# A graph transformer kernel: a longer ring of gathered rows, a step moved from GpSimd to VectorE, and TensorE's first products of the last stage issued earlier

## The reference

```python
for l in range(L):                      # L = 2
    q, k, v = (x @ W[l] + b[l] for each of q, k, v)      # (N, H, D)
    a = (q[dst] * k[src]).sum(-1) * scale
    e = exp(a - segment_max(a, dst)[dst])
    alpha = e / (segment_sum(e, dst)[dst] + 1e-16)
    agg = segment_sum(alpha * v[src], dst)
    x = agg + (x @ Ws[l] + bs[l]) + enc                  # enc: the input x
x = layer_norm(x, ln_g, ln_b)
x = relu(x @ W1 + b1) @ W2 + b2 + x
x = layer_norm(x, ln_g, ln_b)
return _layernorm(x_in + (x + enc))
```

## Time and profile before

| | |
|---|---|
| median of three executions | 2162.43 us |
| the profiled execution | 2160.31 us |
| its span (first to last instruction) | 2158.5 us |
| TensorE, matmuls | 1834.3 us busy, 85% |
| VectorE | 1824.4 us busy, 85% |
| GpSimd | 1446.1 us, 67% |
| ScalarE | 877.4 us, 41% |
| granted TensorE clock, mean | 0.937 of full |
| device memory | 242 GB/s over the span |

### The profile page before, as it was taken

One profiled execution on the slowest core, in us unless ns is written; L12 is line 12 of the kernel. 1 busy time (PEld: TensorE's weight loads), 2 busy tenths in 40 slices (PEclk: granted clock), 3 DMA queues, 4 the chain that ended last, 5 costly groups with the idle time before them and its releaser, 6 DMA issues. The chain is left out here.

```text
span 2158.5 us, 33515 instructions
## 1 busy us (share of the span) xinstructions
PE 1834.3 (85%) x7437; PEld 1392.7 (65%) x7438; DVE 1824.4 (85%) x2304; ACT 877.4 (41%) x2257; POOL 1446.1 (67%) x1417
## 2 busy tenths in 40 slices
PE   6778999998489999997889999957787878888987
PEld 5656666666267787875666666636566666676776
DVE  7659999999899998984999999998898999835554
ACT  3223333333365555552333333334666656532221
POOL 3067777777677777774777777776577777566553
PEclk9989999999699999998999999977999999998998
DMA  7588888888778888886888888886688888763321
GB/s 287 185 270 294 276 287 290 275 284 279 223 225 264 267 265 267 262 265 232 256 285 283 289 279 287 282 264 191 206 281 261 263 263 274 240 190 98 98 69 47
DMA packets 225518, 523.60 MB, mean 243 GB/s; under 512 B 39707, under 2 KB 81563, under 8 KB 225446
## 3 DMA queue, kind: packets, MB, share of 16 engines
q0 software_dynamic: 106624, 349.00, 51.7%
q1 hardware_dynamic: 115942, 168.54, 22.8%
q10 hardware_dynamic: 2880, 5.24, 0.7%
HBM read 446.94 MB, written 75.39 MB: 242 GB/s over the span
## 5 line engine op out<-in xcount | busy, mean ns | idle before, releaser
L850 POOL DMA_INDIRECT all_work<-k_rows,all_work x664 | 632.0, 952 | 217.6 <-issue 188.6
L850 POOL DMA_INDIRECT v_ring<-v_rows,coll_index x624 | 607.6, 974 | 224.5 <-issue 178.2
L1928 PE MATMUL coll_banks<-coll_ev,coll_hot 128*128 128x260 f32 x2656 | 651.3, 393 | 100.4 <-DVE all_work L2049 40.7
L1928 PEld LDWEIGHTS coll_banks<-coll_ev,coll_hot 128*128 128x128 f32 x2656 | 497.1, 193 | 228.6 <-issue 106.1
L1059 PE MATMUL score_q_ps<-score_q,score_hot 128*128 x1328 | 392.6, 420 | 89.2 <-DVE score_q L1099 56.1
L1087 DVE TENSOR_TENSOR all_work<-score_q_ps,all_work 128x1024 f32<-128x1024 f32 x332 | 404.6, 1220 | 38.7 <-PE score_q_ps L1059 20.1
L2035 DVE TENSOR_TENSOR coll_ev<-v_ring,coll_banks 128x1024 f32<-128x1024 f32 x328 | 397.9, 1214 | 11.3 <-DMA v_ring<-v_rows,coll_index 5.1
L1092 DVE TENSOR_REDUCE graph_edge<-all_work 128x1024 f32 (+1 forms) x332 | 397.8, 1209 | 0.0
L1059 PEld LDWEIGHTS score_q_ps<-score_q,score_hot 128*128 128x128 f32 x1328 | 255.6, 199 | 183.4 <-issue 132.7
L1166 ACT ACTIVATE score_hot<-score_local,all_iota_col 128x512 fp32r<-128x512 uint8 x166 | 120.0, 723 | 584.1 <-DVE all_work L1087 548.5
L2049 DVE TENSOR_TENSOR all_work<-all_work,coll_banks 128x520 f32 x354 | 244.5, 691 | 57.6 <-PE coll_banks L1928 46.5
(11 more groups left out here) (323 smaller groups left out, 2340.0 us busy)
## 6 DMA issues: line engine op xcount, KB each, us to landing
score_xt<-x_turned SPq DMA_DIRECT2D x42, 512.0 KB, 6.4
x_turned<-coll_xt SPq DMA_DIRECT2D x40, 512.0 KB, 4.4
all_work<-k_rows,all_work POOLq DMA_INDIRECT x664, 4.9
score_local<-local_dst SPq DMA_DIRECT2D x166, 64.0 KB, 6.5
x_turned<-keys_xt SPq DMA_DIRECT2D x20, 512.0 KB, 4.3
score_skip<-in_x SPq DMA_DIRECT2D x40, 256.0 KB, 4.9
v_rows<-score_v_out SPq DMA_DIRECT2D x40, 256.0 KB, 5.7
skip_rows<-score_skip SPq DMA_DIRECT2D x40, 256.0 KB, 3.8
```

Of the source, the lines that this page charges most:

```text
L850: nc.gpsimd.indirect_dma_start(rows(HALF * turn + s, first)[:, t, :], None, table, at).then_inc(arrived(HALF * turn + s, first), 16)
L1928: last = nc.tensor.matmul(sums[sum_slots[u]][:, part, :], m, ev[:, s % EVS, t, part * AGG // 2:(part + 1) * AGG // 2], start=s == 0 or t = ...
```

## The change

1. The ring of the second layer keeps 16 slots up to step 68 (SWITCH) and has 8 from there on. Which slot and which use a step has is now worked out for each step up to body 5 (STEADY), so VectorE's and ScalarE's bodies 2 to 4 are written out too, and three rounds of four halves on GpSimd. The first layer's ring and order are as they were.
2. W1 is loaded whole at the start of the stage and split in body 4 in place of body 1: ScalarE at steps 7, 9, 11 and 13, VectorE at steps 8, 10, 12 and 14. W2's load moves on SyncE's queue to behind the loop over halves 4 to 15.
3. The order in which the last stage takes the blocks is worked out between bodies 0 and 1, not ahead of body 0.
4. In each half ScalarE has gain and shift at step 5 and the high part at 6, behind the root; VectorE has the low part at 7, behind the inverse root.
5. TensorE goes on to piece 0 of h without a turning ahead of it; blocks 18 and 19 are turned ahead of pieces 1 and 2. ScalarE's first half of W2's high part moves to behind piece 1, the second to behind piece 2, and the gain and shift of block 18 to behind piece 0.
6. Twice x plus shift is one operation of VectorE (scalar_tensor_tensor over 128x2048) ahead of the second pass over a group's first pair, in place of two of GpSimd.

```diff
@@ twice x plus shift
-        def twice_enc(g):
-            pool.wait_ge(enc_in, 16 * GB * (g + 1))
-            nc.gpsimd.tensor_tensor(enc, enc, enc, ALU.add).then_inc(enc_ready, 1)
-            pool.wait_ge(enc_ready, 2 * g + 1)
-            nc.gpsimd.tensor_tensor(enc, enc, across(shift), ALU.add).then_inc(enc_ready, 1)
-            twice_enc(g)
+        def twice_enc(g):
+            dve.wait_ge(enc_in, 16 * GB * (g + 1))
+            v.scalar_tensor_tensor(enc, enc, 2.0, shift.unsqueeze(1).to_broadcast([P, GB, C]), ALU.mult, ALU.add).then_inc(enc_ready, 1)
@@ last_norms
-            dve.wait_ge(enc_ready, 2 * (g + 1))
+            if pair[0] % GB == 0:
+                twice_enc(g)
+            dve.wait_ge(enc_ready, g + 1)
@@ hidden, on TensorE
-                if n == 2:
-                    turn_last()
+                if n in (1, 2):
+                    turn_last(n)
-                    turn(BLOCKS - 2)
-                    mlp.tensor(pe, lambda: turn(BLOCKS - 1))
+                    mlp.tensor(pe, lambda n: turn(BLOCKS - 3 + n))
@@ the ring
-        ring = V_RING if more else HALF
+        SWITCH = V_RING + HEAD + 3 * V_RING
+        def slot_of(n):
+            if n < V_RING:
+                return n
+            return (n - HEAD) % (V_RING if more or n < SWITCH else HALF)
+        STEADY = BODY * (2 if more else -(-SWITCH // BODY))
+        UNROLLED = 1 if more else -(-(SWITCH + HALF) // (2 * V_RING))
@@ SyncE
-                    for i in range(2):
+                    for i in range(KC):
                         load_w1(i)
...
-                    for i in range(2):
-                        sp.wait_ge(w_lo, i + 1)
-                        load_w1(i + 2)
...
-                    sp.wait_ge(w_lo, KC)
-                    sp.dma_start(w2_raw[:], k.W2.rearrange("(c p) n -> p c n", p=P)).then_inc(w2_in, 16)
                     with sp.Fori(1, 4) as it:
                         for turn in range(4):
                             norms_in(4 * it + turn, turn, it)
+                    sp.wait_ge(w_lo, KC)
+                    sp.dma_start(w2_raw[:], k.W2.rearrange("(c p) n -> p c n", p=P)).then_inc(w2_in, 16)
@@ VectorE
-                if not more:
-                    order_of_last_stage()
+                        if not more and weights and h == 1 and at % 2 == 0:
+                            weight_low(at // 4, at // 2 % 2)
-                        if lows[h] and at == 6:
-                            low_part(2 * it + h - (READY + 1), (h + READY + 1) % 2)
+                        if lows[h] and at == 7:
+                            low_part(2 * it + h - (READY + 1), (h + READY + 1) % 2)
                     body(0, (False, False), False)
-                    body(1, (True, True), True, BODY, (False, True))
-                    with dve.Fori(2, LOOPS) as it:
+                    order_of_last_stage()
+                    body(1, (True, True), False, BODY, (False, True))
+                    for it in range(2, STEADY // BODY):
+                        body(it, (True, True), it == STEADY // BODY - 1, BODY, (True, True))
+                    with dve.Fori(STEADY // BODY, LOOPS) as it:
@@ ScalarE
-                        act.wait_ge(ev_dve, weighed_by(V_RING - 1))
+                        act.wait_ge(ev_dve, weighed_by(SWITCH - 1))
+                        if not more and weights and s in (7, 9, 11, 13):
+                            weight_high((s - 7) // 4, (s - 7) // 2 % 2)
-                        if not more and highs[h] and at == 3:
+                        if not more and highs[h] and at == 5:
                             gain_and_shift(half - (READY + 1))
-                        if highs[h] and at == (0 if more else 4):
+                        if highs[h] and at == (0 if more else 6):
                             high_part(half - (READY + 1), (h + READY + 1) % 2, 16 * (it - 2 + h))
+                    high_part(j - 2, 1, stored - 16)
                     root(j - 1)
-                    mlp.w2_high(act, 0)
                     normalise(j - 1)
-                    gain_and_shift(j - 1)
-                    high_part(j - 1, 0, stored)
-                    def normal_rows():
+                    def turned_and_normal():
+                        gain_and_shift(j - 1)
+                        high_part(j - 1, 0, stored)
                         root(j)
                         normalise(j)
                     def turned_rows():
                         gain_and_shift(j)
                         high_part(j, 1, stored)
-                        mlp.w2_high(act, 1)
-                    mlp.scalar(act, (normal_rows, turned_rows))
+                        mlp.w2_high(act, 0)
+                    mlp.scalar(act, (turned_and_normal, turned_rows, lambda: mlp.w2_high(act, 1)))
```

More of the change, by code:

```diff
@@ L826, in side_product, with gather_rows @@
     return nc.tensor.matmul(out, xt[:, a, c, :], w[b][:, c, :], start=c == 0 and n == 0, stop=False)
-def gather_rows(nc, k, pool, table, rows, sources, index, held, first_index, wait_index, asked, arrived, rows_used, used, steps, begun=0):
+def gather_rows(nc, k, pool, table, rows, sources, index, held, first_index, wait_index, asked, arrived, rows_used, used, steps,
+                begun=0, unrolled=0):
     n = HALF * TPS
@@ L841, in gather_half @@
         for s in range(n_steps):
-            count = used(half, turn, times, s)
+            count = used(turn, times, s)
             if not isinstance(count, int) or count > 0:
@@ L846, in gather_half @@
             pool.sem_inc(asked, 1)
-            first = isinstance(times, int) and times == 0
             for t in range(TPS):
                 at = bass.IndirectOffsetOnAxis(ap=index[:, turn, s * TPS + t:s * TPS + t + 1], axis=0)
-                nc.gpsimd.indirect_dma_start(rows(HALF * turn + s, first)[:, t, :], None, table, at
-                                             ).then_inc(arrived(HALF * turn + s, first), 16)
-    for turn in range(begun, turns if begun else 0):
-        gather_half(turn, turn, 0)
-    with pool.Fori(1 if begun else 0, halves // turns) as it:
+                nc.gpsimd.indirect_dma_start(rows(turn, times, s)[:, t, :], None, table, at).then_inc(arrived(turn, times, s), 16)
+    for times in range(unrolled):
+        for turn in range(begun if times == 0 else 0, turns):
+            gather_half(turns * times + turn, turn, times)
+    with pool.Fori(unrolled, halves // turns) as it:
         for turn in range(turns):
@@ L915, in _ @@
             def _(pool):
-                gather_rows(nc, k, pool, k.k_d, lambda n, first: rows[:, n % RING], k.src_t[:], index, 1, first_index,
-                            lambda half, turn, times: pool.wait_ge(index_ready, half + 1), asked, lambda n, first: k.k_in[n % RING], multiplied, lambda half, turn, times, s: HALF * half + s + 1, SCORE_STEPS)
+                gather_rows(nc, k, pool, k.k_d, lambda turn, times, s: rows[:, (HALF * turn + s) % RING], k.src_t[:], index, 1, first_index,
+                            lambda half, turn, times: pool.wait_ge(index_ready, half + 1), asked,
+                            lambda turn, times, s: k.k_in[(HALF * turn + s) % RING], multiplied,
+                            lambda turn, times, s: HALF * (2 * times + turn) + s + 1, SCORE_STEPS)
                 pool.wait_ge(v_stored, 16 * (BLOCKS + 1))
@@ L2057, in weight_low @@
                         hi, lo = (part[:, 2 * m + i] for part in w1)
-                        source = w1_raw[:, i]
+                        source = w1_raw[:, 2 * m + i]
                     v.tensor_tensor(lo, source, hi.bitcast(F32), ALU.subtract).then_inc(w_lo, 1)
@@ L2352, in _ @@
                     act.wait_ge(columns_in, 16 * 3)
-                    body(1, (False, True), none, True, BODY, both)
-                    with act.Fori(2, LOOPS) as it:
+                    body(1, (False, True), none, False, BODY, both)
+                    for it in range(2, STEADY // BODY):
+                        body(it, both, none, it == STEADY // BODY - 1, BODY, both)
+                    with act.Fori(STEADY // BODY, LOOPS) as it:
                         body(it, both, none, False, BODY, both)
```

73 lines of the change are left out of this document (42 added, 31 removed).

## The result

The changed kernel takes 2142.99 us (median of four executions, 2139.14 to 2143.57), the kernel before 2161.51 beside it: a ratio of 0.991, with a 95% interval of 0.989 to 0.993. That is 18.5 us faster; 2137 was forecast, with 2122 to 2152 as the range. The profiled execution took 2143.26 us, 2141.4 of it span.

What follows compares the result with a forecast made beforehand. VectorE was taken to set the pace in the second collection, TensorE, with waits for h, in the last stage. Terms: 2160.3 - 4.0 - 2.8 - 13.0 - 5.1 + 1.0 = 2136.4, said as 2137; range 2122 to 2152.

Steps and rivals of the forecast that it cites:

- the collection: Second layer's collection: ring, last stage's order, W1's splitting, written-out bodies and order inside a half, together -4.0 us.
- Ring: Second collection, 16 slots up to step 68: GpSimd's 20.70 us stall goes, but nobody waited for the rows, 0.
- Order of the last stage: Working out the block order behind body 0: -0.9 and +1.6, together +0.7 us, bounds -0.9 and +1.7.
- Written-out bodies: Bodies 2 to 4 in the collection: three fewer passages round the loop at 0.39 us each on VectorE, -1.1 us.
- W1's splitting: Moved from body 1 to body 4: body 1 loses 7.3 us, body 4 takes over 4.6 and most stall; -1.8, bounds -5 and +1.
- Order inside a half: Collection, later gain, high part and low part: row scale known up to 0.6 us sooner; -1.8 for eight bodies, bounds -8 and +4.
- rival of the falling clock: Collection: the high part ahead of step 7's copy widens TensorE's gap, clock falls in every half, +39 us, 2175; chance 0.04.
- The point between 1.01 and 2.54: Collection: length in us of a TensorE gap from which the clock was expected to fall, somewhere between these two.
- Hand-over: From the last sums to the first h: TensorE goes on without its 3.82 us wait; -2.8 us, bounds -4.0 and 0.
- Groups 1 to 3: Last stage: the 2.80 us wait and low clock go, 44.7 us a group; -13.0 us, bounds -8 and -15.
- Group 0: Last stage's first group: GpSimd's second gain-and-b2 pair still overlaps VectorE; -5.1 of the 9.74 us wait, bounds -2 and -8.
- Tail: Group 4 at the end: VectorE's added 2.28 us operation less 1.22 to spare, +1.0 us.

Runs made afterwards that it cites:

- w1_first_body_2: The changed kernel with the second layer's ring 8 slots deep from step 20 and W1 split in body 1, only body 1 written out: 2142.17 us, ratio 0.9912.
- before_early_read: The kernel before with only ScalarE's register read moved to step 0 of a half: 2156.69 us, ratio 0.9975.
- order_back_2: The changed kernel with gain, high part and low part put back to steps 3, 4 and 6 of a half: 2129.21 us, ratio 0.9861.
- early_read_2: The changed kernel with ScalarE's register read at step 0 of a half, not step 1: 2125.40 us, ratio 0.9836; early_read, its first run in a disturbed time, 2642.81.

## Why the prediction was right, and where it was not

The time (2137 forecast, 2143 measured) and the direction were right, the direction by the mechanism of the last stage, the closeness of the sum by luck, since terms missed on both sides: the collection by 8.6 us the one way, the last stage and hand-over together (-25.5 against -19.9) by 5.6 the other; 3.8 more of the profiled execution lie ahead of the change.

*Ring*: 0, not contradicted. GpSimd's stall went, and w1_first_body_2, in which GpSimd stands still for 19.94 us again, is as fast. But in before_early_read, with a ring of 8 and faster bodies, VectorE does wait for rows (8.7 us), so the 0 holds for this pace alone. *Order of the last stage*: the nine operations run from 1514.55 to 1516.38, 1.8 us where 1.7 was said; the first weighing came 0.6 sooner, 0.9 was said. From the carried column to the start of body 1 both kernels take 51.4: 0 in place of +0.7. *Written-out bodies*: -1.1, right. In order_back_2 four of VectorE's seven gaps of 0.36 to 0.39 at the loop's borders are left; in the changed kernel none shows.

*W1's splitting*: -1.8 with a bound of -5; by its own words (a stall of 2.8 less 1, on top of the 4.6) the sum would have been -0.9. Body 1 lost 8.8. In order_back_2 body 4 exceeds its neighbours (38.3 and 39.4) by 3.6, in early_read_2 (37.2 and 37.5) by 4.0, less than the 4.6 of bare work: the stall that the prediction carried over to body 4 didn't come along. That makes about -5, a term mis-sized by 3; not all of it is the move, since body 1 with the splitting in it also takes 41.38 and not 46.41. All of items 1 to 3 together were forecast at -2.2 and gave -7.1 in order_back_2.

*Order inside a half*: **the step that failed**: -1.8 with bounds -8 and +4, measured +10.6 by the ratios, +13.8 by the medians. The prediction followed the high part up to the copy for step 7, and there it was right: the 1.01 of the earlier trace rows became 1.5. It said of a TensorE gap that grows that the clock decides, and then took the wrong gap. The one that mattered was at step 2 of a body's second half, 1.67 to 2.66, behind the read: a stretch of ScalarE's idle time that the view of waits books under "issue" and that the prediction never asked about. Its rival of the falling clock had the right mechanism, once a body and not 16 times at step 7; the price of one such fall was sized rightly (2.45 said; VectorE's wait rose from 1.24 to 3.82).

The point between 1.01 and 2.54 from which a gap was to lower the clock doesn't exist as such: the length of the gap alone doesn't decide. The kernel before has a gap of 1.93 ahead of the first products of each body from 3 on. Behind four of these eight the next eight products took 1.99 (the granted clock of the two stretches is 1.00 and 0.57, third from the end), behind four 2.75 to 3.64:

```profile
1715.91 1.99 PE L1928 MATMUL coll_banks<-coll_ev,coll_hot 128*128 128x260 f32 x8 [1.93 <-DVE all_work L2049]
...
1754.93 7.18 PE L1928 MATMUL coll_banks<-coll_ev,coll_hot 128*128 128x260 f32 x24 [1.93 <-DVE all_work L2049]
```

```profile
1715.90:1717.90 2.00, 1.99 (x8) 1.42 (x8) 1.58 (x3) 1.68 (x5) 1.70 (x2) 1.00 1.02 344
1754.90:1758.30 3.40, 3.37 (x9) 2.69 (x10) 2.07 (x3) 2.81 (x7) 2.68 (x3) 0.57 0.92 318
```

And in order_back_2 gaps of 2.56 and 2.93 were followed by 1.99. That this first gap of a body gets shorter was said rightly: at 1714.42 in the changed kernel it is 1.27, with the clock up behind it.

*Hand-over*: -2.8, measured -4.1, at the bound. The chain of 8.0 us is as long as its parts say, plus 1.00 for the store out of the only buffer of rows, which the working left out; the gain wasn't lost in the clock afterwards, which was the reason for taking less than 4.

*Groups 1 to 3*: -13.0, measured -15.2, just past the bound of -15. The wait went, as said (GpSimd's pair ended 1.2 us ahead of VectorE's; 1.2 was said, though the times given there, 1990.13 and 1989.3, make 0.9); the 1.1 us a group left for slow stretches and the fifth h weren't there: 43.5 to 44.2 is 192 products by 0.227. *Group 0*: -10.9 less the 4.1 of the hand-over leaves -6.8, where -5.1 was said. The lock still shuts one operation out:

```profile
1938.50 6.24 DVE L1397 SCALAR_TENSOR_TENSOR coll_xt<-coll_xt,coll_z_mean_var,graph_edge 128x512 f32<-128x512 f32 x2
1944.67 2.28 DVE L1373 SCALAR_TENSOR_TENSOR all_work<-all_work,graph_edge 128x2048 f32<-128x2048 f32 x1
...
1956.18 0.50 PE L166 MATMUL coll_banks<-mlp_yt_hi,v_ring 128*128 128x512 f32 x1 [2.39 <-ACT mlp_h_hi L1449]
```

The two begin at 1938.50 and end at 1944.74; GpSimd's operation beside them ends at 1944.19, and by that the second got through only then. 9.74 of waiting became 2.39. *Tail*: +1.0, measured +0.6.

The rule of the Trainium skill (SBUF — State Buffer, Who interferes with whom) that such operations exclude each other fits the 6.24 of group 0 and the 1.42 in group 1. The warning of the Trainium skill in Perfetto Trace Analysis, Optimizing Scalar/DVE Operations, that offloading between these two might not help, doesn't decide here: moving work from GpSimd to VectorE gives 20.5 of the 25.5 us behind the last add.

Left open: how a store ahead of it lengthens the read, and what besides the gap decides on TensorE's clock.

## What to carry to other kernels

An edit that reorders an engine's queue is priced at every place where another engine waits for that queue, the idle times under "issue" included: a wait of 1.7 us that costs one can be 0.9 us away from one behind which the clock is low and the next engine waits 2.6 us longer. Reads of registers belong where their engine has to wait anyway, ahead of that wait, and not right behind a large store: here that was worth 17.6 us. When a sum of small terms comes out right, compare term by term before believing any of them.

## What the runs showed of the hardware

A read of eight numbers from SBUF into ScalarE's registers took 0.54 to 0.57 us where no store of rows had been issued in the 3 us before it (70 reads, most with an operation of ScalarE in work), 0.63 to 1.37 behind one store of 256 KB (38 reads), and 0.83 to 2.38 behind this and one of 512 KB (61 reads).

TensorE's eight products took 1.99 us at a granted clock of 1.00 (2.4 GHz). In the changed kernel they took 1.99 behind gaps of 1.47 to 1.85 and 2.6 to 3.8 behind seven of the eight gaps of 2.5 to 2.8 (0.54 granted over the stretch at 1742.60, so for most of it the lower level, 1.2 GHz); in the kernel before, gaps of 1.93 were followed by either.

Two VectorE operations of 512 columns with two inputs in SBUF took 1.42 us with GpSimd idle, and 6.24 to 9.95 beside GpSimd's operations of 2048 columns.

In the disturbed time the kernel before took 24 to 25% longer; early_read's last stage, which gathers nothing, kept the distances of early_read_2 (44.16, 43.54, 44.16) to 0.01 us.
